# Attention row sums: six adding transfers and two row-sum parts a group, an earlier V and an earlier inverse

## The reference, cut to what matters

```
xn  = layernorm(x)
q, k, v = split(xn @ qkv_w.T + qkv_b)          # 16 heads of 32
p   = softmax(q @ k.T * 32**-0.5)              # (4, 16, 2048, 2048)
att = (p @ v) @ proj_w.T + proj_b
out = x + att + ffn(xn)                        # two picked experts per batch element, gelu
```

## Time and profile before

| | |
|---|---|
| time, median of 3 runs | 4841.46 us (4841.42 to 4845.11) |
| the profiled execution, its own time | 4836.55 us |
| its span | 4834.7 us |
| PE busy | 4691.4 us, 97% of the span |
| POOL busy | 3223.0 us, 67% |
| DVE busy | 3170.4 us, 66% |
| ACT busy | 2398.9 us, 50% |
| granted PE clock over the span | 0.987 |

### The profile page before, as it was taken

One profiled execution on the slowest core, in us unless ns is written; L12 is line 12 of the kernel. 1 busy time (PEld: TensorE's weight loads), 2 busy tenths in 40 slices (PEclk: granted clock), 3 DMA queues, 4 the chain that ended last, 5 costly groups with the idle time before them and its releaser, 6 DMA issues. The chain is left out here.

```text
span 4834.7 us, 66456 instructions
## 1 busy us (share of the span) xinstructions
PE 4691.4 (97%) x24396; PEld 2773.0 (57%) x24396; DVE 3170.4 (66%) x5296; ACT 2398.9 (50%) x4653; POOL 3223.0 (67%) x1117
## 2 busy tenths in 40 slices
PE   8999999999899999999999999999999999999979
PEld 6887878878654444444444444444444444444447
DVE  4223232333188888888888888888888888888534
ACT  2111121121146666666666666666666666666621
POOL 1121212121249998989989989999899998998920
PEclk9999999999979999999999999999999999999989
DMA  5344343343346655656656566665665656655466
GB/s 172 103 127 122 109 138 102 119 129 111 91 106 130 137 127 125 138 125 137 133 124 139 124 131 136 126 139 120 132 137 124 140 125 132 137 124 121 90 225 236
DMA packets 254215, 633.49 MB, mean 131 GB/s; under 512 B 45252, under 2 KB 79044, under 8 KB 212936
## 3 DMA queue, kind: packets, MB, share of 16 engines
q0 software_dynamic: 36864, 268.45, 27.8%
q1 hardware_dynamic: 217032, 360.85, 27.0%
HBM read 224.96 MB, written 134.74 MB: 74 GB/s over the span
## 5 line engine op out<-in xcount | busy, mean ns | idle before, releaser
L927 DVE TENSOR_REDUCE unit_max<-mx_ps 128x1 f32<-128x512 f32 x4096 | 2535.2, 681 | 317.0 <-PE mx_ps L1002 310.9
L836 POOL TENSOR_TENSOR p_pair<-p_sb 128x2048 f32<-128x2048 f32 x512 | 2439.8, 4811 | 185.3 <-PE mx_ps L1026 128.3
L913 ACT ACTIVATE p_sb<-st_ps 128x512 f32<-128x512 f32 x4096 | 2061.9, 628 | 905.5 <-PE st_ps L1073 905.5
L1002 PE MATMUL mx_ps<-k_x,q_x 96*128 96x512 f32 x4096 | 1684.9, 415 | 21.5 <-DMA k_x<-k_lo_d 19.6
L1073 PE MATMUL st_ps<-q_x,k_x 97*128 97x512 f32 x4096 | 1607.8, 413 | 37.9 <-ACT p_sb L913 37.3
L1073 PEld LDWEIGHTS st_ps<-q_x,k_x 97*128 97x128 f32 x4096 | 770.3, 188 | 599.3 <-ACT p_sb L913 512.8
L1002 PEld LDWEIGHTS mx_ps<-k_x,q_x 96*128 96x128 f32 x4096 | 784.6, 192 | 456.7 <-DVE unit_max L927 234.3
L1014 PE MATMUL o_ps<-p_sb,v_sb 128*32 128x512 f32 x8192 | 986.8, 599 | 0.0
L285 POOL TENSOR_TENSOR h_lo<-h_f,h_hi 128x512 fp32r<-128x512 f32 x128 | 165.2, 1291 | 687.7 <-DVE h_hi L469 687.7
L1014 PEld LDWEIGHTS o_ps<-p_sb,v_sb 128*32 128x32 f32 x8192 | 214.0, 109 | 494.1 <-ACT p_sb L913 309.8
L469 DVE CAST h_hi<-h_f 128x512 fp32r<-128x512 f32 x128 | 55.0, 431 | 541.9 <-ACT h_f L342 541.9
(11 more groups left out here) (94 smaller groups left out, 3926.8 us busy)
## 6 DMA issues: line engine op xcount, KB each, us to landing
p_pair<-p_pair POOLq DMA_DIRECT2D x256, 1024.0 KB, 7.3
q_x<-q_hi_d SPq DMA_DIRECT2D x128, 256.0 KB, 8.6
k_x<-k_hi_d SPq DMA_DIRECT2D x68, 256.0 KB, 7.3
xt<-x SPq DMA_DIRECT2D x64, 256.0 KB, 2.7
stage<-w SPq DMA_DIRECT2D x32, 512.0 KB, 5.1
q_hi_d<-qk_hi SPq DMA_DIRECT2D x64, 256.0 KB, 3.0
q_lo_d<-qk_lo SPq DMA_DIRECT2D x64, 256.0 KB, 3.9
k_hi_d<-qk_hi SPq DMA_DIRECT2D x64, 256.0 KB, 2.6
```

The lines of the kernel that those rows point to most:

```text
L836: pool.tensor_tensor(p_pair[:, slot, :, :], p_sb[:, n % SLOTS, :, :], p_sb[:, (n + 1) % SLOTS, :, :], ALU.add).then_inc(pair_done, 1)
L913: act.activation(p_sb[:, (L * G * KT + n) % SLOTS, h, :], st_ps[bank(g, m)][:, :], ACT.Exp, scale=SCALE).then_inc(exp_done, 1)
L927: dve.reduce_max(unit_max[:, n // 4, n % 4:n % 4 + 1], mx_ps[UNIT_PLACE[n] % RING][:, :], AX.X).then_inc(bank_read, 1)
L1002: pe.matmul(mx_ps[UNIT_PLACE[n] % RING][:, :], q_x[qc][0:R, h, t * P:(t + 1) * P], k_x[u][0:R, h, kc * 512:(kc + 1) * 512], start=True, st ...
```

## The change

- `pair_slots` takes two layouts in turn instead of a rotation.
- A group's eight pair sums are gathered by six adding transfers into two slots, a and b. Each slot has its own semaphore: `joined[0]` for a, `joined[1]` for b, `joined[2]` for c. L874, POOL's own addition at the end of a group, goes.
- The last adding transfer of a group (`last_join`) is issued in the next group, behind its first pair.
- `PARTS` has two entries instead of three, both in the next group: slot a in step 0, slot b at the end of step 3.
- The step strings change: two U items move from in front of the third score to the end of the step, and V comes right behind the third score.
- In SP's queue `spread_inverse` moves ahead of `load_shift`.
- `normalise`, which stood between pair 6 (behind `join(d, c)`) and pair 7, now stands between pair 5 (behind `join(b, d)`) and pair 6.

```diff
     def pair_slots(group):
-        a, b, c, d = 0, 1, 2, 3
-        for _ in range(group):
-            a, b, c, d = c, b, d, a
-        return a, b, c, d
-    NA, NJ = NP + 1, 4
-    PARTS = [(2, 0, False, 7), (4, 0, True, 10), (0, NA, False, 11)]
+        return (0, 1, 2, 3) if group % 2 == 0 else (0, 3, 2, 1)
+    NA = NP
+    PARTS = [(2, 0, 8), (2, 1, 11)]
...
-        STEPS = ["USUSUSUVUSSUSUSUS", "USUSUSUVUSSUSUSUS", "USUSUSUVZUSSUSUSUS", "USUSUSUVZUSSUSUSUS",
-                 "USUSUSUVUSSUSUSUS", "USUSUSUVUSSUSUSUS", "USUSUSUVTUSSUSUSUS", "USUSUSUVZUSSUSUSUS"]
+        STEPS = ["SUSUSVZUSSUSUSUSUU", "SUSUSVUSSUSUSUSUU", "SUSUSVUSSUSUSUSUU", "SUSUSVUSSUSUSUSUUZ",
+                 "SUSUSVUSSUSUSUSUU", "SUSUSVUSSUSUSUSUU", "SUSUSVTUSSUSUSUSUU", "SUSUSVUSSUSUSUSUU"]
...
                             spread_sums(read_count(L, g, PART_PLACE[LAST_PART], first, last))
+                        if not (first and g == 0):
+                            spread_inverse(L * G + g)
                         if not (last and g == G - 1):
                             load_shift(L * G + g + 2, (qc + 1) % QC)
                         if not (first and g == 0):
-                            spread_inverse(L * G + g)
                             store_group(L, it - 1 if qc == 0 else it, (qc - 1) % QC, L * G + g)
...
                 def group(at):
                     a, b, c, d = pair_slots(at)
                     if at > 0:
-                        pool.wait_ge(joined, at * NJ * 16)
+                        pool.wait_ge(sum_done, at * NS - 1)
                     pair(at, 0, a)
-                    pool.wait_ge(pair_done, at * NA)
+                    if at > 0:
+                        last_join(at - 1)
                     pair(at, 1, b)
                     pool.wait_ge(pair_done, at * NA + 2)
-                    join(a, b)
+                    join(a, b, joined[0])
                     if at > 0:
-                        pool.wait_ge(sum_done, at * NS - 1)
+                        pool.wait_ge(joined[1], at * 32)
                     pair(at, 2, c)
                     if at > 0:
                         pool.wait_ge(sum_done, at * NS)
                     pair(at, 3, d)
-                    pool.wait_ge(pair_done, at * NA + 3)
-                    pool.wait_ge(joined, (at * NJ + 1) * 16)
-                    join(a, c)
+                    pool.wait_ge(pair_done, at * NA + 4)
+                    join(c, d, joined[2])
+                    pool.wait_ge(joined[0], at * 32 + 16)
                     pair(at, 4, b)
-                    pool.wait_ge(pair_done, at * NA + 5)
-                    pool.wait_ge(joined, (at * NJ + 2) * 16)
-                    join(d, b)
-                    pair(at, 5, c)
-                    pool.wait_ge(sum_done, at * NS + 1)
-                    pair(at, 6, a)
+                    pool.wait_ge(joined[2], at * 32 + 16)
+                    join(a, c, joined[0])
+                    pair(at, 5, d)
                     pool.wait_ge(pair_done, at * NA + 6)
-                    pool.wait_ge(joined, (at * NJ + 3) * 16)
-                    join(d, c)
+                    join(b, d, joined[1])
                     if at > 0:
                         normalise(at)
-                    pair(at, 7, b)
-                    pool.wait_ge(pair_done, at * NA + NP)
-                    pool.tensor_tensor(p_pair[:, a, :, :], p_pair[:, a, :, :], p_pair[:, b, :, :], ALU.add).then_inc(pair_done, 1)
+                    pool.wait_ge(joined[0], at * 32 + 32)
+                    pair(at, 6, c)
+                    pool.wait_ge(joined[1], at * 32 + 16)
+                    pair(at, 7, d)
+                    pool.wait_ge(pair_done, at * NA + 8)
+                    join(c, d, joined[2])
+
+                def last_join(at):
+                    _, b, c, _ = pair_slots(at)
+                    pool.wait_ge(joined[2], at * 32 + 32)
+                    join(b, c, joined[1])
...
                 def sums(L, g, i, place):
-                    joins, adds, in_d, at = PARTS[i]
-                    slot = pair_slots(L * G + g)[3 if in_d else 0]
-                    if joins:
-                        pe.wait_ge(joined, ((L * G + g) * NJ + joins) * 16)
-                    else:
-                        pe.wait_ge(pair_done, (L * G + g) * NA + adds)
+                    joins, part, at = PARTS[i]
+                    slot = pair_slots(L * G + g)[part]
+                    pe.wait_ge(joined[part], (L * G + g) * 32 + joins * 16)
```

More of the change, by code:

```diff
@@ L641, in attention_stage @@
         bank_read, max_done, inv_done, o_done = sem("bank_read"), sem("max_done"), sem("inv_done"), sem("o_done")
-        pair_done, joined = sem("pair_done"), sem("joined")
+        pair_done = sem("pair_done")
+        joined = [sem(f"joined_{slot}") for slot in "abc"]
         sum_ld, inv_st, inv_ld = sem("sum_ld"), sem("inv_st"), sem("inv_ld")
@@ L648, in attention_stage @@
         SK = 4 * KT
-        STEPS = ["USUSUSUVUSSUSUSUS", "USUSUSUVUSSUSUSUS", "USUSUSUVZUSSUSUSUS", "USUSUSUVZUSSUSUSUS",
-                 "USUSUSUVUSSUSUSUS", "USUSUSUVUSSUSUSUS", "USUSUSUVTUSSUSUSUS", "USUSUSUVZUSSUSUSUS"]
+        STEPS = ["SUSUSVZUSSUSUSUSUU", "SUSUSVUSSUSUSUSUU", "SUSUSVUSSUSUSUSUU", "SUSUSVUSSUSUSUSUUZ",
+                 "SUSUSVUSSUSUSUSUU", "SUSUSVUSSUSUSUSUU", "SUSUSVTUSSUSUSUSUU", "SUSUSVUSSUSUSUSUU"]
         FIRST = sum(s.count("U") for s in STEPS[AHEAD:])
-        PARTS_AT = [at for _, _, _, at in PARTS]
+        PARTS_AT = [at for _, _, at in PARTS]
         FILLS = [(j, i, step) for j in range(NP) for i, step in enumerate(STEPS[j]) if step in "UTZ"]
@@ L837, in pair, with join @@
                                        ALU.add).then_inc(pair_done, 1)
-                def join(into, slot):
-                    pool.dma_start(p_pair[:, into, :, :], p_pair[:, slot, :, :], accum_op=ALU.add).then_inc(joined, 16)
+                def join(into, slot, landed):
+                    pool.dma_start(p_pair[:, into, :, :], p_pair[:, slot, :, :], accum_op=ALU.add).then_inc(landed, 16)
                 def group(at):
@@ L856, in group @@
                     pair(at, 3, d)
-                    pool.wait_ge(pair_done, at * NA + 3)
-                    pool.wait_ge(joined, (at * NJ + 1) * 16)
-                    join(a, c)
+                    pool.wait_ge(pair_done, at * NA + 4)
+                    join(c, d, joined[2])
+                    pool.wait_ge(joined[0], at * 32 + 16)
                     pair(at, 4, b)
-                    pool.wait_ge(pair_done, at * NA + 5)
-                    pool.wait_ge(joined, (at * NJ + 2) * 16)
-                    join(d, b)
-                    pair(at, 5, c)
-                    pool.wait_ge(sum_done, at * NS + 1)
-                    pair(at, 6, a)
+                    pool.wait_ge(joined[2], at * 32 + 16)
+                    join(a, c, joined[0])
+                    pair(at, 5, d)
                     pool.wait_ge(pair_done, at * NA + 6)
-                    pool.wait_ge(joined, (at * NJ + 3) * 16)
-                    join(d, c)
+                    join(b, d, joined[1])
                     if at > 0:
                         normalise(at)
-                    pair(at, 7, b)
-                    pool.wait_ge(pair_done, at * NA + NP)
-                    pool.tensor_tensor(p_pair[:, a, :, :], p_pair[:, a, :, :], p_pair[:, b, :, :], ALU.add).then_inc(pair_done, 1)
+                    pool.wait_ge(joined[0], at * 32 + 32)
[8 more added lines that the diff above has]
+                    join(b, c, joined[1])
                 for at in range(NQ * QC):
                     group(at)
+                last_join(NQ * QC - 1)
                 normalise(NQ * QC)
@@ L1097, in sum_parts @@
                                 pe.wait_ge(shift_done, L * G + G)
-                            for i, (_, _, _, at) in enumerate(PARTS):
+                            for i, (_, _, at) in enumerate(PARTS):
                                 if at == (j if mine else j + NP):
@@ L1123, in _ @@
                 for i in range(NS):
-                    if PARTS[i][3] >= NP:
-                        sums(TURNS - 1, G - 1, i, PART_PLACE[PARTS[i][3]])
+                    if PARTS[i][2] >= NP:
+                        sums(TURNS - 1, G - 1, i, PART_PLACE[PARTS[i][2]])
 def output_stage(nc, proj_wT, o_d, y_d, out):
```

## The result

The changed kernel takes 4962.26 us (median, 4957.96 to 4966.9), the kernel before 4843.28 us beside it: ratio 1.0244, 95% interval 1.0232 to 1.0257. It is 2.4% slower. The direction was forecast; the size was not: +119 us against +32, and 27 us above the range.

The account below looks back on a forecast made before the run. POOL's ring of four bare landings was taken as the bound: 62 x (51.0 - 50.61) plus 7.9 us for the ends makes +32 us, so 4873 us; the 8-in-10 range was 4785 to 4935 us.

Parts of the forecast that it names:

- POOL's ring: POOL's queue and its transfers form a closed loop with four bare landings L: 4L + 21.37, 51.0 us a group.
- Five segments: POOL's group from issue to issue, starting at the second join(c, d): 7.92, 16.95, 7.92, 5.82 and 12.38 us.
- the two prices read from single rows: On POOL, from a landing to the waiting issue 0.52 us, from a landing to a waiting pair 0.11 us.
- Which L? ... I take 7.4: Time from a join's issue to its landing, one value for all four: 7.4 us, bounds 7.05 and 7.7.
- rival B: Second join(c, d) collides with SP's loads, landing after 9 us on average: group 52.2 us, +106 us, 4948 us; chance 0.16.
- normalise and pair 6 at 6.74 us: POOL's queue behind join(b, d): issue, normalise and pair 6 fill 0.62 + 1.24 + 4.88 us before pair 7.
- The strings at nothing: PE's changed order of step items priced at 0, bounds 0.8 us a group either way.
- PE's stall for normalise gone: At the fourth exponential ACT's copy should find the earlier normalise done: up to -0.8 us a group for PE.
- The late shift: SP reaches the shift roughly 2 us later, with 2 us in hand: 0, at most 0.5 us a group of PE wait.
- Ends: First group -6.5 us without L874 and a wait, tail +14.4 us for the last transfers; together +7.9 us.
- The four waits of POOL: POOL waits at last_join 2.4, pair 2 1.1, join(a, c) 2.4 and pair 7 0.8 us, some 6.7 us a group.
- rival D: POOL's ring has one landing too many, so PE stays the bound at 48.95 us a group: -95 us, 4746 us; chance 0.12.

Follow-up runs that it names:

- e1: Changed kernel with every adding transfer moving two of the four heads (512 KB instead of 1 MB): 4748.1 us, ratio 0.981 to the kernel before.
- e5: Changed kernel with SP loading only an eighth of the key columns from the third set of heads on: 4879.1 us, ratio 1.0087.
- e6: Changed kernel with normalise back behind pair 6 instead of in front of it: 5079.4 us, ratio 1.0493.
- e4: Kernel before with only the step strings of the change, its three Z items kept right behind V: 4807.6 us, ratio 0.9933.
- e7: Changed kernel with the step strings of the kernel before, Z items where the change has them: 4974.3 us, ratio 1.0278.
- e3: Kernel before with only spread_inverse moved ahead of load_shift and normalise between pair 5 and pair 6: 4891.1 us, ratio 1.0108.
- e8: Kernel before with new strings, inverse ahead of shift, normalise between pairs 5 and 6, SP's store and loads held until pair 7: 4792.1 us, ratio 0.99.
- e9: e8 with the inverse's four loads parted from its write, behind the shift and the landing of join(a, c): 4828.6 us, ratio 0.997.

## Why the prediction was wrong

- **POOL's ring is the bound: right.** Five segments were forecast, and each is in the timeline. e1 shows that it is the landings: with them at 4.6 us PE paces again, at 49.20 us a group (48.95 forecast for PE alone). Of the two prices read from single rows, that from a landing to a pair stood (0.11 us, measured 0.08). That from a landing to an issue did not carry over: 0.52 us was right for the kernel before (median 0.54), but in the changed kernel it is 0.29, a mean of 0.32, at two places of the ring. So -0.4 us a group, 25 us, which hid part of what follows.
- **"Which L? ... I take 7.4": the step that failed.** One mean was taken for four landings at four different places. Over groups 2 to 61 those of `last_join` and the first `join(c, d)` are 7.2 us, better than 7.4, and that of `join(b, d)` is covered by the next point. That of the second `join(c, d)`, behind normalise and SP's loads, is 8.9 us on average and 11.8 in every fourth group: +1.5 us a group, some 90 us. That is rival B, given 0.16, with 4948 us against the measured 4962; e5 makes the key loads small and gets 4879. That B's total came so near is in part luck: it had the same short last segment and the same high price of an issue. Its own evidence was in the earlier trace rows. The argument against it, that the steady state reached no more than 8.7 us, was about another order of issue: there the join went out first. The change moves normalise, and so SP's loads, from behind the join to the front of the next one. The prediction said that the loads would fall there, but left that out of the sum.
- **normalise and pair 6 at 6.74 us: too short.** POOL waits 1.5 us (80.8 / 55) for the inverse, after which pair 7 seldom has to wait for `join(b, d)` (0.16 us on average). SP's side was walked for the shift alone. The last segment is 13.17 instead of 12.38: +0.8 us a group, 49 us, in part made good by the shorter landings and the cheaper issue. No run isolates this term: e6 took the wait away, but put the loads elsewhere.
- **The strings at nothing: mis-sized, inside the bounds.** -0.55 us a group by e4 where PE paces; in the changed kernel at most 12 us (e7), which the forecast did not need.
- **PE's stall for normalise gone: right.** ACT's wait on L829 is no longer in the list. Alone it brought nothing (e3), since the order of transfers changed with it.
- **The late shift: right in size.** 13.3 us of PE in 57 groups, while POOL is the bound; what it cost was not measured by itself.
- **Ends: right.** First group -6.8 us against -6.5, tail +14.5 against +14.4 (its terms add up to 14.5). The later beginning of the attention and the output stage, together +6 us, had no term.
- **The four waits of POOL** were forecast at 6.7 us a group; for transfers they are 344 / 57 = 6.0, with the inverse 7.5. DMA share 0.79 (0.82), PE's share 96% (95%).

By the rule of the Trainium skill that the prediction weighed (DMA: Bandwidth & Descriptors, section on the anatomy of one DMA on the gpsimd path; an estimate of 4.4 us a transfer of 1 MB) PE would have stayed the bound, as in rival D. The trace does not agree: the adding transfers of 1 MB took 6.9 us or more after the change as well, and those of 512 KB in e1 4.5 us or more.

## What to carry to other kernels

Before work is moved from an engine to transfers, walk the issuing queue and count the landings on which something waits at once: that closed ring bounds the period whatever the other engines do. Price each landing by its own place, by what another queue has issued in the microseconds ahead of it, not by the median. And when an instruction moves that another queue waits for, follow that queue to the loads that it releases; a gain on one engine (0.8 us here) can send 2 MB ahead of a transfer that is waited for.

## What was not expected of the hardware

- An adding transfer of 1 MB with nothing big ahead of it landed after 7.2 us on average (`last_join` of the changed kernel, 7.0 to 8.5). With 2.25 MB of loads issued 2.6 us behind it the mean was 7.7 us (`join(d, c)` of the kernel before, every fourth group). With those loads begun 4 to 8 us ahead of it, it took 11.5 to 12.8 us (changed kernel), and with them at the same moment 14.1 on average and up to 15.6 (e3).
- With half the bytes it took 4.6 us (e1, median), and still 10.5 to 12.1 with the loads begun 2 us ahead.
- Four loads of 64 KB issued beside such a transfer made it 8.5 us on average instead of 7.4 (e8 against the kernel before); with them held back it was 7.7 (e9).
- From the landing of a transfer to POOL's next issue of one that waited for it passed 0.54 us in the kernel before and 0.29 in the changed one (medians).
- PE idle for 5.6 us came back with a granted clock of 0.60 over the next 10 us; in the kernel before, without such stalls, it was 1.00 over the 3000 us of the earlier trace rows.
